# Attention on one Trainium2 core: where a group's first blocks and the multiply by the reciprocals stand

## The chip, the cores and the metric

The kernel runs on one core of a Trainium2 chip. Five engines work with queues of their own and meet at semaphores: TensorE (PE), VectorE (DVE), ScalarE (ACT), GpSimd (POOL) and SyncE (SP), which issues most DMAs. The metric is device time in microseconds (us), the median of several runs.

## The reference, cut to what matters

Three layers follow each other, each with a residual: half a mixture-of-experts feed-forward network, attention, and half a feed-forward network again. The change is in the attention.

```python
x = L0_attn_x                                     # (2, 2048, 512)
x = x + 0.5 * ffn(layernorm(x), ...)
x = x + attn(layernorm(x), Wq, bq, Wk, bk, Wv, bv, Wo, bo)
x = x + 0.5 * ffn(layernorm(x), ...)

def attn(x, ...):                                 # 16 query heads of 32, one head of keys and values
    q = (x @ Wq + bq).reshape(b, s, 16, 32).transpose(0, 2, 1, 3)
    k = x @ Wk + bk
    v = x @ Wv + bv
    scores = einsum('bhsd,btd->bhst', q, k) / sqrt(32)
    out = einsum('bhst,btd->bhsd', softmax(scores, axis=-1), v)
    return out.transpose(0, 2, 1, 3).reshape(b, s, 512) @ Wo + bo
```

## The kernel before

The attention works on 32 groups: 8 chunks of 512 queries (QT) by 4 groups (GPC) of 4 heads (HG). G counts the groups, g is the place in the chunk. For a group the keys come in 16 steps of 128 (STEPS), taken as 8 pairs (PAIRS).

What one group does:

- **PE, scores** (L1562): for each step and head a 128x512 matmul into one of three banks of pS. ACT takes the exponential of each (L1520) into prob. `scores` for the first step of a group waits until the shifts have been copied into qT.
- **PE, values** (L1600): for each step four matmuls into pO, when its four exponentials are done. The first of a group waits until pO has been copied out (semaphore s_oc).
- **POOL, pair sums** (L1461): adds the exponentials of two steps, and its DMAs (L1477) add these sums in acc. PE adds acc over the keys (`denominators`, pair 3).
- **The shifts.** A softmax needs the maximum of each row before the exponentials. While group G is computed, PE makes the score blocks of group G+1 a second time, in the other layout (`maxima`, L1575, 64 blocks of 128x512). I call them **blocks**. Each goes to one of the 4 banks of pM (RING), and DVE reduces it to its row maxima (L1716); PE may be four blocks ahead of DVE and no more. When all 64 are done, DVE makes the shifts (`make_shifts`, L1727 to L1731), PE transposes them into bank 2 of pM (`transposed_shifts`, L1591), and DVE and ACT copy two heads each into qT (`copy_shift`, L1738 and L1525). The third block of a group waits for these copies, since it reuses the bank.
- **The reciprocals.** DVE copies the sums out of PSUM (`copy_d`, pair 3, L1748). SP writes them to DRAM and reads them back as 128x16; DVE takes the reciprocals (`reciprocals`, behind the blocks of pair 5, RECIPROCAL_PAIR, L1754); SP writes them to DRAM and reads them back broadcast into d_rec, by four DMAs of 64 KB (L1399). All this is for the group before, G-1. Then POOL multiplies the copied values by d_rec (`normalise`, L1490), behind its last pair sum of the group.
- **The values' copy.** DVE copies pO (`copy_o`, L1743) at the start of the next group, behind its first two blocks (EARLY).
- **The output.** In the second group of each chunk but the first, PE multiplies the chunk before by Wo, in four parts behind pairs 1, 2, 4 and 6 (`output`, L1584), and DVE adds each to x (L1721). I call these the output groups; there are 7.

The order of PE is written out by hand. AT_HEAD says behind which of the first eight scores of a group a block stands (the first score comes with the seam), AT_PAIR how many blocks are among the eight scores issued in pair p, for the steps of pair p+1. EARLY blocks of a group come ahead of its first score, at the end of the group before. Each engine's queue is in order. So a waiting instruction holds everything behind it on its engine. `chunks` runs chunks 1 and 2, and chunks 4 to 6, as loops, and the others as straight code; the loops turn three times in all.

## Time and profile before

| | |
|---|---|
| median of 3 runs | 3292.02 us (3288.11 to 3294.11) |
| the profiled execution's own time | 3288.66 us |
| its span, first to last instruction | 3286.9 us |
| busy: PE, DVE, ACT, POOL | 2812.6, 2045.0, 1481.8, 2210.8 us |
| attention, transposes of the first group to the last's | from 833.0 to 2520.9 us |
| L1716, reductions of blocks (DVE) | 1984 of 680 ns, 1210.8 us busy |
| L1575 and L1562, blocks and scores (PE) | 1984 and 2048, 808.3 and 842.0 us busy |
| L1490, multiply by the reciprocals (POOL) | 31, 1302 ns the median |
| PE idle at the transposes (L1591), ended by DVE's shift | 17.1 us in 25 waits |
| POOL idle before L1490, ended by the DMA of d_rec | 19.2 us in 19 waits |

The span is cut into 40 slices on the page; slices 11 to 31 are the attention's. Busy matmuls overlap their neighbours in the records, so a distance between starts says more of PE than a duration. An idle time stands in brackets with what ended it: "[0.44 <-DVE attention_shift L1731]" is 0.44 us without work, ended by that instruction of DVE.

### The profile page before, as it was taken

What the parts mean: (1) busy time and instruction counts of PE and PEld (TensorE: products, weight loads), DVE (VectorE), ACT (ScalarE), POOL (GpSimd) and SP (SyncE); (2) the same over time, 40 slices, a digit from 0 to 9 for tenths busy, and PEclk for the clock granted to TensorE, in tenths of its full rate; (3) what the DMA queues carried; (4) which work ended last, traced back from release to release, by engine and by line L of the source; (5) the groups of instructions that cost most, each with busy time, mean ns of one, the idle gap of its engine ahead of it and who ended that gap; (6) DMA issues with size and microseconds to landing.
All of it is one profiled execution on the core that took longest, in us unless ns stands there. A gap on an engine that the chain in (4) does not pass through costs nothing. (4 is left out here: it accounts for less than half of the span.)

```text
span 3286.9 us, 50812 instructions
## 1 busy us (share of the span) xinstructions
PE 2812.6 (86%) x15136; PEld 1579.5 (48%) x15136; DVE 2045.0 (62%) x3940; ACT 1481.8 (45%) x2815; POOL 2210.8 (67%) x1392
## 2 busy tenths in 40 slices
PE   7967778398899999999999999999999798777760
PEld 4644444176555454555554544455554355444430
DVE  7943222267788787788787877777875397222222
ACT  3422222153666565566565655665656243222210
POOL 2148888462688787788887877877878222788870
PEclk9989887699999999999999999999999898879885
DMA  6479999894577676676776766757766243999998
GB/s 215 167 210 249 235 243 232 191 278 158 113 161 142 136 159 140 142 153 131 166 142 135 159 138 139 156 116 155 144 124 142 89 166 116 245 235 245 235 197 315
DMA packets 217011, 576.36 MB, mean 175 GB/s; under 512 B 33948, under 2 KB 34972, under 8 KB 192792
## 3 DMA queue, kind: packets, MB, share of 16 engines
q0 software_dynamic: 87296, 343.98, 52.0%
q1 hardware_dynamic: 125208, 220.55, 20.5%
q10 hardware_dynamic: 4224, 8.39, 0.7%
q8 instruction: 137, 2.24, 0.3%
q14 instruction: 146, 1.20, 0.1%
HBM read 230.94 MB, written 155.24 MB: 117 GB/s over the span
## 5 line engine op out<-in xcount | busy, mean ns | idle before, releaser
L1716 DVE TENSOR_REDUCE attention_mx<-attention_pM 128x1 f32<-128x512 f32 x1984 | 1210.8, 680 | 208.7 <-PE attention_pM L1575 192.6
L1520 ACT ACTIVATE attention_prob<-attention_pS 128x512 f32<-128x512 f32 x2048 | 1035.0, 631 | 565.9 <-PE attention_pS L1562 471.3
L1461 POOL TENSOR_TENSOR attention_pair<-attention_prob 128x1024 f32<-128x1024 f32 x380 | 949.5, 2507 | 195.6 <-ACT attention_prob L1520 184.0
L1562 PE MATMUL attention_pS<-attention_qT,prep_kT 128*128 128x512 f32 x2048 | 842.0, 417 | 25.3 <-issue 16.7
L1575 PE MATMUL attention_pM<-prep_kT,attention_qT 96*128 96x512 f32 x1984 | 808.3, 410 | 0.0
L1562 PEld LDWEIGHTS attention_pS<-attention_qT,prep_kT 128*128 128x128 f32 x2048 | 389.2, 191 | 365.8 <-issue 178.0
L1600 PE MATMUL attention_pO<-attention_prob,attention_v 128*32 128x512 f32 x4096 | 492.5, 598 | 0.0
L629 POOL DMA_INDIRECT sum<-experts_res,c_table x256 | 403.7, 1577 | 106.7 <-issue 76.6
L1575 PEld LDWEIGHTS attention_pM<-prep_kT,attention_qT 96*128 96x128 f32 x1984 | 378.5, 192 | 110.4 <-DVE attention_mx L1716 44.4
L755 DVE TENSOR_SCALAR experts_res<-experts_pD,experts_rows 128x512 f32<-128x512 f32 x128 | 90.7, 747 | 422.5 <-DMA sum<-experts_res,c_table 277.3
L658 PE MATMUL experts_pT<-c_ident,experts_rows 128*128 128x128 f32 x1024 | 186.3, 325 | 189.9 <-issue 69.4
L613 POOL DMA_INDIRECT experts_rows<-xn_rows,c_table x256 | 250.0, 976 | 103.0 <-issue 70.7
L658 PEld LDWEIGHTS experts_pT<-c_ident,experts_rows 128*128 128x128 f32 x1024 | 146.4, 211 | 235.5 <-issue 103.3
L1461 POOL TENSOR_TENSOR prep_acc<-attention_prob 128x1024 f32<-128x1024 f32 x68 | 165.2, 2582 | 132.1 <-ACT attention_prob L1520 132.1
L672 PE MATMUL experts_pU<-experts_xT,experts_wup 128*64 128x256 f32 x2048 | 245.6, 394 | 8.3 <-DVE experts_xT L739 8.1
L717 ACT ACTIVATE experts_res<-experts_pD,experts_rows 128x512 f32<-128x512 f32 x128 | 82.3, 684 | 321.1 <-DMA sum<-experts_res,c_table 281.0
L1600 PEld LDWEIGHTS attention_pO<-attention_prob,attention_v 128*32 128x32 f32 x4096 | 107.0, 109 | 244.1 <-issue 134.5
L672 PEld LDWEIGHTS experts_pU<-experts_xT,experts_wup 128*64 128x64 f32 x2048 | 148.0, 143 | 145.6 <-issue 84.7
L270 POOL TENSOR_TENSOR route_eqp<-route_eq,route_count 128x1536 f32<-128x1536 bf16 x16 | 52.1, 3259 | 212.5 <-ACT route_count L376 212.5
L685 PE MATMUL experts_pD<-experts_wdn,experts_hid 64*128 64x512 f32 x512 | 186.8, 866 | 4.8 <-DVE experts_hid L747 3.9
L739 DVE COPY experts_xT<-experts_pT 128x512 f32<-128x512 f32 x128 | 88.1, 688 | 158.5 <-PE experts_pT L658 88.9
L1461 POOL TENSOR_TENSOR attention_acc<-attention_prob 128x1024 f32<-128x1024 f32 x64 | 156.0, 2604 | 28.3 <-ACT attention_prob L1520 28.3
(161 smaller groups left out, 2695.2 us busy)
## 6 DMA issues: line engine op xcount, KB each, us to landing
prep_acc<-attention_pair POOLq DMA_DIRECT2D x96, 1024.0 KB, 7.7
attention_acc<-attention_pair POOLq DMA_DIRECT2D x90, 1024.0 KB, 7.6
experts_wup<-in_L_ffn_w_up_dram SPq DMA_DIRECT2D x128, 256.0 KB
attention_qT<-q_parts SPq DMA_DIRECT2D x96, 256.0 KB
xn_rows<-route_xn SPq DMA_DIRECT2D x16, 1152.0 KB, 6.7
sum<-route_sh SPq DMA_DIRECT2D x16, 1024.0 KB, 4.4
experts_wdn<-in_L_ffn_w_down_dram SPq DMA_DIRECT2D x64, 256.0 KB
q_parts<-prep_acc SPq DMA_DIRECT2D x64, 256.0 KB, 4.4
```

Of the source, the lines that this page charges most:

```text
L613: pool.indirect_dma_start(rows[e % RING][:, a * HALVES + h, :], None, xn_d, bass.IndirectOffsetOnAxis(ap=k["table"][:, 2 * e + a, h:h + 1] ...
L629: pool.indirect_dma_start(sums[a], bass.IndirectOffsetOnAxis(ap=k["table"][:, 2 * e + a, h:h + 1], axis=0), res[e % 2][:, a, h, :], None, ...
L658: t = pe.transpose(pT[:, half, o:o + P], rows[e % RING][:, a * HALVES + h, c:C:CK], k["ident"][:, :])
L672: t = pe.matmul(pU[b][a * H:(a + 1) * H, v, :], wup[b][:, a, c, v * H:(v + 1) * H], xT[b][:, c, a, :], start=c == 0, stop=c == CK - 1)
L685: pe.matmul(pD[:, h, a, :], hid[b][own, h * P:(h + 1) * P], wdn[b][own, :], start=True, stop=True).then_inc(s_dn[a], 1)
L755: dve.tensor_scalar(res[e % 2][:, 1, h, :], pD[:, h, 1, :], rows[e % RING][:, HALVES + h, C + 2 * e + 1:C + 2 * e + 2], None, ALU.mult).th ...
L1461: pool.tensor_tensor(to[:, part], prob[2 * n % PROBS][:, part], prob[(2 * n + 1) % PROBS][:, part], ALU.add).then_inc(s_pair, 1)
L1520: act.activation(prob[t % PROBS][:, h * QT:(h + 1) * QT], pS[:, at, :], ACT.Exp).then_inc(s_ex, 1)
L1562: pe.matmul(pS[:, at, :], kT[:, key:key + P], qT[g][:, h, :], start=True, stop=True).then_inc(s_sc, 1)
L1575: pe.matmul(pM[:, r % RING, :], qT[g][0:3 * DH, h, t * P:(t + 1) * P], kT[0:3 * DH, key:key + 512], start=True, stop=True).then_inc(s_mp, 1)
L1600: ins = pe.matmul(pO[h * DH:(h + 1) * DH, :], v_sb[:, batch * STEPS + t, :], prob[t % PROBS][:, h * QT:(h + 1) * QT], start=t == 0, stop=t ...
L1716: dve.tensor_reduce(mx[:, unit, part:part + 1], pM[:, r % RING, :], X, ALU.max).then_inc(s_mr, 1)
```

## The change

Three things change, in the attention alone.

1. The order of blocks. Four blocks (EARLY) stand ahead of a group's first score, two of them directly behind the transposes and so ahead of the last two steps' values, two behind these values. The head has four blocks and not six; pairs 4 and 5 have nine and pair 6 has six.
2. ACT copies the values (`copy_o`), between its copies of the shifts and the next group's first exponential.
3. DVE multiplies by the reciprocals (`normalise`), behind its copies of the shifts and ahead of the next group's first block. POOL does so no more.

The wait for Wo's load moves to its first use.

```diff
-        EARLY = 2
-        AT_HEAD = (0, 0, 1, 1, 1, 1, 1, 1)
-        AT_PAIR = (8, 8, 8, 8, 8, 8, 8, 0)
+        EARLY = 4
+        AT_HEAD = (0, 0, 0, 0, 1, 1, 1, 1)
+        AT_PAIR = (8, 8, 8, 8, 9, 9, 6, 0)
...
@@ gpsimd
-                            if last and n == STEPS // 2 - 2:
-                                normalise(c, g - 1)
...
-                            normalise(c, g - 1)
...
@@ scalar
+                def copy_o(G, g):
+
+                    act.wait_ge(s_pv, A + (G + 1) * STEPS)
+                    act.activation(o_raw(g)[:, :], pO[:, :], ACT.Copy).then_inc(s_oc, 1)
...
                             for h in (2, 3):
                                 copy_shift(G + 1, (g + 1) % GPC, h)
+                            copy_o(G, g)
                             for h in range(HG):
                                 exponential(G + 1, 0, h)
...
@@ tensor
                             two_steps(0, 2 * p + 2, () if last else range(AT_PAIR[p]))
+                            if not last and AT_PAIR[p] > 2 * HG:
+                                maxima(base, r, n, nxt, ahead, G)
+                                n, r = n + 1, r + 1
                         elif not last:
 
                             transposed_shifts(G + 1)
+                            if not before_last:
+                                early(*follower, range(2))
...
-                            early(c + 1 if nxt == 0 else c, nxt, 1 if end else ahead)
+                            early(*follower, range(2, EARLY))
                         scores(G + 1, nxt, 0, 0, ahead)
...
@@ vector
+                def normalise(c, g):
+
+                    G = GPC * c + g
+                    dve.wait_ge(s_oc, A + G + 1)
+                    dve.wait_ge(s_ri, A + 64 * (G + 1))
+                    dve.tensor_tensor(o_n[g][:, :], o_raw(g)[:, :], d_rec[:, :], ALU.mult).then_inc(s_on, 1)
...
-                    if not first:
-                        copy_o(c if g else c - 1, (g - 1) % GPC)
...
                         make_shifts(G + 1, base + r)
                         for h in range(2):
                             copy_shift(G + 1, (g + 1) % GPC, h)
+                    if not first:
+                        normalise(c if g else c - 1, (g - 1) % GPC)
```

PE at the seam between two groups, before. L1575 are blocks (pM), L1562 scores (pS), L1600 values (pO), L1591 the transposes:

```order
L1562 MATMUL attention_pS<-attention_qT,prep_kT 128x512
L1575 MATMUL attention_pM<-prep_kT,attention_qT 128x512
L1600 MATMUL attention_pO<-attention_prob,attention_v 32x512 x8
L1591 MATMUL attention_pM<-c_ident,attention_shift 128x128 x4
L1600 MATMUL attention_pO<-attention_prob,attention_v 32x512 x8
L1575 MATMUL attention_pM<-prep_kT,attention_qT 128x512 x2
L1562 MATMUL attention_pS<-attention_qT,prep_kT 128x512 x3
L1575 MATMUL attention_pM<-prep_kT,attention_qT 128x512
```

The same place now (the lines are L1561, L1548, L1587 and L1578):

```order
L1548 MATMUL attention_pS<-attention_qT,prep_kT 128x512 x2
L1587 MATMUL attention_pO<-attention_prob,attention_v 32x512 x8
L1578 MATMUL attention_pM<-c_ident,attention_shift 128x128 x4
L1561 MATMUL attention_pM<-prep_kT,attention_qT 128x512 x2
L1587 MATMUL attention_pO<-attention_prob,attention_v 32x512 x8
L1561 MATMUL attention_pM<-prep_kT,attention_qT 128x512 x2
L1548 MATMUL attention_pS<-attention_qT,prep_kT 128x512 x5
L1561 MATMUL attention_pM<-prep_kT,attention_qT 128x512
```

The last scores ahead of the transposes have no blocks between them, two blocks come ahead of the last values and two behind, and five scores follow without a block.

DVE from the copy of the sums of one group to that of the next, before:

```order
L1748 COPY attention_d<-attention_pM 128x512
L1716 TENSOR_REDUCE attention_mx<-attention_pM 128x1 x16
L1754 RECIPROCAL attention_d_in<-attention_d_in 128x16
L1716 TENSOR_REDUCE attention_mx<-attention_pM 128x1 x8
L1727 TENSOR_REDUCE attention_pM<-attention_mx 128x16
L1728 TENSOR_REDUCE attention_shift<-attention_mx 128x16
L1731 TENSOR_TENSOR attention_shift<-attention_pM,attention_shift 128x16
L1738 CAST attention_qT<-attention_pM 32x512 x2
L1716 TENSOR_REDUCE attention_mx<-attention_pM 128x1 x2
L1743 COPY attention_o_n<-attention_pO 128x512
L1716 TENSOR_REDUCE attention_mx<-attention_pM 128x1 x38
```

And now:

```order
L1737 COPY attention_d<-attention_pM 128x512
L1710 TENSOR_REDUCE attention_mx<-attention_pM 128x1 x18
L1743 RECIPROCAL attention_d_in<-attention_d_in 128x16
L1710 TENSOR_REDUCE attention_mx<-attention_pM 128x1 x6
L1721 TENSOR_REDUCE attention_pM<-attention_mx 128x16
L1722 TENSOR_REDUCE attention_shift<-attention_mx 128x16
L1725 TENSOR_TENSOR attention_shift<-attention_pM,attention_shift 128x16
L1732 CAST attention_qT<-attention_pM 32x512 x2
L1750 TENSOR_TENSOR attention_o_n<-attention_o_n,attention_d_rec 128x512
L1710 TENSOR_REDUCE attention_mx<-attention_pM 128x1 x40
```

Six reductions and not eight stand between the reciprocals and the shifts; the copy behind the next group's second block is gone, and the multiply with d_rec stands ahead of all of that group's reductions.

## Rows read from the trace of the kernel before

**Rows 1.** The page: the clock granted to PE in 40 slices, in tenths.

```profile
PEclk9989887699999999999999999999999898879885
```

**Rows 2.** Timeline, PE: start, us, engine, line, operation, count, idle before and releaser.

```profile
2355.96 0.66 PE L1591 MATMUL attention_pM<-c_ident,attention_shift 128*128 128x128 f32 x4 [0.43 <-DVE attention_shift L1731]
...
2394.03 0.51 PE L1562 MATMUL attention_pS<-attention_qT,prep_kT 128*128 128x512 f32 x1
...
2397.97 1.92 PE L1600 MATMUL attention_pO<-attention_prob,attention_v 128*32 128x512 f32 x16
2399.83 0.50 PE L1562 MATMUL attention_pS<-attention_qT,prep_kT 128*128 128x512 f32 x1
...
2403.77 1.92 PE L1600 MATMUL attention_pO<-attention_prob,attention_v 128*32 128x512 f32 x16
2406.13 0.66 PE L1591 MATMUL attention_pM<-c_ident,attention_shift 128*128 128x128 f32 x4 [0.44 <-DVE attention_shift L1731]
...
2409.15 0.86 PE L1562 MATMUL attention_pS<-attention_qT,prep_kT 128*128 128x512 f32 x3
...
2410.23 0.51 PE L1562 MATMUL attention_pS<-attention_qT,prep_kT 128*128 128x512 f32 x1
...
2417.45 1.07 PE L1600 MATMUL attention_pO<-attention_prob,attention_v 128*32 128x512 f32 x8
```

**Rows 3.** Timeline, DVE, in the same group.

```profile
2399.60 0.24 DVE L1754 RECIPROCAL attention_d_in<-attention_d_in 128x16 f32<-128x16 f32 x1
2400.60 4.87 DVE L1716 TENSOR_REDUCE attention_mx<-attention_pM 128x1 f32<-128x512 f32 x8 [0.76 <-PE attention_pM L1575]
...
2405.89 0.18 DVE L1731 TENSOR_TENSOR attention_shift<-attention_pM,attention_shift 128x16 f32<-128x16 f32 x1
2406.83 1.40 DVE L1738 CAST attention_qT<-attention_pM 32x512 fp32r<-32x512 f32 x2 [0.75 <-PE attention_pM L1591]
2409.11 1.29 DVE L1716 TENSOR_REDUCE attention_mx<-attention_pM 128x1 f32<-128x512 f32 x2 [0.88 <-PE attention_pM L1575]
2410.32 0.68 DVE L1743 COPY attention_o_new<-attention_pO 128x512 f32<-128x512 f32 x1
```

**Rows 4.** Timelines of three groups: reciprocals (DVE), last pair sum and multiply (POOL).

```profile
1302.71 0.24 DVE L1754 RECIPROCAL attention_d_in<-attention_d_in 128x16 f32<-128x16 f32 x1
1314.24 1.30 POOL L1490 TENSOR_TENSOR attention_o_n<-attention_o_n,attention_d_rec 128x512 f32<-128x512 f32 x1 [1.68 <-DMA attention_d_rec<-d_parts]
...
1518.00 0.24 DVE L1754 RECIPROCAL attention_d_in<-attention_d_in 128x16 f32<-128x16 f32 x1
1527.51 1.39 POOL L1490 TENSOR_TENSOR attention_o_n<-attention_o_n,attention_d_rec 128x512 f32<-128x512 f32 x1
...
2406.59 2.67 POOL L1461 TENSOR_TENSOR attention_pair<-attention_prob 128x1024 f32<-128x1024 f32 x1
2409.75 1.30 POOL L1490 TENSOR_TENSOR attention_o_n<-attention_o_n,attention_d_rec 128x512 f32<-128x512 f32 x1 [0.48 <-DMA attention_d_rec<-d_parts]
2412.90 2.39 POOL L1461 TENSOR_TENSOR attention_acc<-attention_prob 128x1024 f32<-128x1024 f32 x1 [1.85 <-ACT attention_prob L1520]
```

**Rows 5.** Timelines of an output group: reciprocals (DVE) and transposes (PE).

```profile
1794.29 0.24 DVE L1754 RECIPROCAL attention_d_in<-attention_d_in 128x16 f32<-128x16 f32 x1
...
1803.91 0.66 PE L1591 MATMUL attention_pM<-c_ident,attention_shift 128*128 128x128 f32 x4
```

**Rows 6.** Windows behind a loop turn: stretch, length, PE busy, PEclk, DMA, GB/s.

```profile
1254.80:1261.60 6.80, 3.45 (x8) 0.50 0.81 157
1261.60:1265.10 3.50, 1.82 (x8) 0.99 0.01 2
1265.10:1268.50 3.40, 3.40 (x10) 0.50 0.00 0
```

**Rows 7.** Timelines of the stage before, a DVE and a POOL addition.

```profile
659.72 1.73 POOL L1033 TENSOR_TENSOR attentionp_got<-attentionp_got,prep_bo 128x512 f32<-128x512 f32 x1
660.88 1.14 DVE L1162 TENSOR_TENSOR attentionp_got<-attentionp_got,attentionp_other 128x512 f32<-128x512 f32 x1
```

More of the change, by code:

```diff
@@ L1432, in _ @@
             def _(pool):
-                begin(pool, s_pair, s_on)
+                begin(pool, s_pair)
                 def add_pair(c, g, n):
@@ L1478, in bring @@
                                    ).then_inc(s_acc[g % 2][n % 2], 16)
-                def normalise(c, g):
-                    G = GPC * c + g
-                    pool.wait_ge(s_oc, A + G + 1)
-                    pool.sem_inc(k["pool_on"], 1)
-                    pool.wait_ge(s_ri, A + 64 * (G + 1))
-                    pool.sem_inc(k["pool_on"], 1)
-                    if g == 0 and not (isinstance(c, int) and c == 0):
-                        pool.wait_ge(s_mr, A + items_before(c, 2))
-                        pool.sem_inc(k["pool_on"], 1)
-                    pool.tensor_tensor(o_n[g][:, :], o_raw(g)[:, :], d_rec[:, :], ALU.mult).then_inc(s_on, 1)
                 def body(c, batch):
@@ L1496, in body @@
                             add_pair(c, g, n)
-                            if last and n == STEPS // 2 - 2:
-                                normalise(c, g - 1)
-                        if last:
-                            continue
-                        if g > 0:
-                            normalise(c, g - 1)
-                        elif not (isinstance(c, int) and c == 0):
-                            normalise(c - 1, GPC - 1)
                 chunks(body)(pool)
@@ L1509, in _ @@
             def _(act):
-                begin(act, s_ex, s_sha)
+                begin(act, s_ex, s_oc, s_sha)
                 def exponential(G, t, h):
@@ L1581, in output @@
                     if t == 0:
+                        pe.wait_ge(s_wo, A + 16)
                         pe.wait_ge(s_on, A + GPC * (c + 1))
@@ L1634, in last_output, with early @@
                         ins.then_inc(s_mp, 1)
-                def early(c, g, ahead):
+                def early(c, g, ahead, blocks):
                     nxt = (g + 1) % GPC
                     pe.wait_ge(s_q[nxt], A + 48 * (c + (2 if nxt == 0 else 1)))
-                    for n in range(EARLY):
+                    for n in blocks:
                         maxima(items_before(c, g), n, n, nxt, ahead, GPC * c + g)
@@ L1651, in group @@
                     ahead = 1 if static and c == CHUNKS // 2 - 1 and nxt == 0 else batch
+                    before_last = static and c == CHUNKS - 1 and nxt == GPC - 1
+                    turn = static and c == CHUNKS // 2 - 1 and nxt == GPC - 1
+                    follower = (c + 1 if nxt == 0 else c, nxt, 1 if turn else ahead)
                     base = items_before(c, g)
@@ L1682, in group @@
                     if not last:
-                        if not (static and c == CHUNKS - 1 and nxt == GPC - 1):
-                            end = static and c == CHUNKS // 2 - 1 and nxt == GPC - 1
-                            early(c + 1 if nxt == 0 else c, nxt, 1 if end else ahead)
+                        if not before_last:
+                            early(*follower, range(2, EARLY))
                         scores(G + 1, nxt, 0, 0, ahead)
@@ L1693, in _ @@
                 transposed_shifts(0)
-                early(0, 0, 0)
+                early(0, 0, 0, range(EARLY))
                 scores(0, 0, 0, 0, 0)
-                pe.wait_ge(s_wo, A + 16)
                 chunks(body)(pe)
@@ L1710, in _ @@
             def _(dve):
-                begin(dve, s_mr, s_mx, s_shift, s_shd, s_dc, s_rec, s_oc, s_lrec, s_lon)
+                begin(dve, s_mr, s_mx, s_shift, s_shd, s_dc, s_rec, s_on, s_lrec, s_lon)
                 def maxima(base, r, n):
@@ L1738, in copy_shift @@
                     dve.tensor_copy(qT[g][3 * DH:4 * DH, h, :], pM[h * DH:(h + 1) * DH, 2, :]).then_inc(s_shd, 1)
-                def copy_o(c, g):
-                    dve.wait_ge(s_pv, A + (GPC * c + g + 1) * STEPS)
-                    dve.tensor_copy(o_raw(g)[:, :], pO[:, :]).then_inc(s_oc, 1)
                 def copy_d(base, r, G):
```

## The prediction, made before the changed kernel was timed

> **What bounds the kernel now.** I read the page first. TensorE (PE) is busy nine tenths or more of nearly every slice of the attention stage, and its clock is 0.9 to 1.0 there [rows 1]. So I looked for PE's idle time and asked who ends it, by the timeline of one group.
>
> A group has 64 score matmuls and 64 "blocks" (matmuls for the next group's row maxima, each of which DVE must reduce), eight pairs of steps, and a seam. I measure everything from the shifts' transposes, called T. They start at 2355.96 and 2406.13: 50.17 us a group [rows 2]. A pair of steps takes 5.80 us (2394.03 to 2399.83): 3.94 for 16 matmuls, or 0.24 an item, and 1.86 for the values (2397.97 to 2399.83). DVE needs (4.87 - 0.68) / 7 = 0.60 us for a reduction in a row of eight [rows 3], so a pair costs it 4.8: PE is the bound there and DVE catches up during the values.
>
> Two places are different.
> - At T, PE waits. Its last values start at 2403.77 and take 1.86, so it could transpose at 2405.63; it does so at 2406.13, 0.50 later, idle until DVE's shift [rows 2, 3].
> - Behind T, DVE is the bound. Values 14 and 15, two blocks and the first score come by T + 3.02. DVE starts on the blocks at T + 2.98 (2409.11), copies the values at 2410.32, and the next values of PE start at T + 11.32 (2417.45) [rows 2, 3]. PE is four blocks ahead at most (the ring), so those values come when DVE is through 12 reductions and the copy: 13 turns of 0.60 after 2409.11 is 2416.9, and another 0.5 for the last block and the switch. The row says 8.34 from DVE's first reduction to PE's values.
>
> **The change, part by part.**
>
> *Blocks out of the last pair.* Two fewer at pair 6, one more at each of pairs 4 and 5. PE's sum stays. Before T, both engines shift: PE starts pair 6 at 2399.83 + 0.24 and is at T after 3.94 - 0.48 + 1.86, at 2405.39. DVE begins pair 6's reductions at 2400.60 + 0.24 and needs six: 5 x 0.60 + 0.68 to 2404.5, then 0.60 for the shifts (2405.48 to 2406.07) [rows 3]: 2405.1. The shifts are ready in time and the 0.50 wait goes. The ninth block costs no wait: its ring place is free after five reductions.
>
> *The reciprocals slide towards T.* DVE takes them behind pair 5's ninth reduction: 0.60 later, 2400.20. So T is 5.2 us behind them, not 6.5 (2399.60 to 2406.13).
>
> *The multiply goes from POOL to DVE, behind the shift copies and ahead of all blocks.* This decides. The multiply waits for four transfers that SP issues once the reciprocals are done, through DRAM. POOL's multiply starts 10.15 us behind them in this group, 0.48 of it waiting for that DMA; the earliest of the ordinary groups is 9.51 (1518.00 to 1527.51), the latest 11.53 (1302.71 to 1314.24) [rows 4]. Over the 19 ordinary groups that have blocks behind the seam (not behind an output group, not at a loop's turn) the mean is 10.37. POOL could afford that. DVE has its shift copies done at T + 2.1 (2408.23) [rows 3] and then stands until T + 10.37 - 5.2 = T + 5.2, with two, then four blocks waiting in PSUM. The multiply takes a turn of 0.60, taken from the copy of the same size that it replaces; DVE's first reduction starts at T + 5.8, against T + 2.98.
>
> PE passes four blocks unhindered (the ring), and four scores without blocks. Its fifth block needs one reduction done, at T + 5.8 + 0.68, and PE is there at T + 3.02 + 0.48 (two more items) + 1.08 (2409.15 to 2410.23) + 0.48 + 0.24 = T + 5.3: it waits some 1.2 us, and from there on DVE paces it. The next values need 12 reductions and now no copy: 8.34 - 0.60 = 7.74 behind the first, T + 13.5. That is 2.2 us later than 11.32. Less the 0.50 at T, an ordinary group loses 1.7 us; 19 x 1.7 = **+32 us**. No later pair gives it back, since PE bounds those.
>
> *Seven seams in output groups.* There the output's matmuls lie between, so T is 9.62 us behind the reciprocals (1794.29 to 1803.91) [rows 5]. Now 8.8 (0.60 less, and 0.24 less of PE). With the ordinary groups' 9.5 to 11.5 the multiply could start at T + 0.7 to T + 2.7, and DVE asks for it at T + 2.1. DVE would allow the values at T + 2.7 + 7.74 = 10.4; An exponential, and with it a score, comes each 0.48 at best (PE's two items; from a score to the next there ACT is no faster), so score 15 comes at T + 3.5 + 1.08 + 12 x 0.48 and the values 0.66 later (the last block, and the switch), at T + 11.0: 0.3 gained. T itself had no wait there. 7 x 0.3 = -2.
>
> *Three loop turns.* Behind such a seam PE is busy 3.45 of 6.8 us, and the clock is at 0.50 [rows 6]: it stands on the branch and then runs at half speed, which hides DVE's delay. Only the wait at T goes: -1.5. The first seam has no multiply (-0.9). The last seam has no blocks: the 0.50 goes, and ACT's copy gives it back.
>
> *ACT's copy of the values.* 0.6 us, between the shift copies and the next exponential. The last values end near T + 3.4 and the first exponential is at T + 3.4 (2409.58) today, T + 3.9 then: hidden at the cost of at most 0.1, taken as nothing. It takes the copy off DVE, which is counted above.
>
> *POOL's multiply (1.3 us) goes.* POOL then waits for ACT 1.85 us anyway [rows 4]: nothing.
>
> *Interference of DVE and POOL.* A DVE addition of two 128x512 SBUF tiles takes 1.14 us beside POOL's addition of the same shape [rows 7]; DVE's copy of that shape takes 0.68 [rows 3]. Were the multiply beside POOL's additions it would cost 0.46 more, 9 us over 19 groups. But POOL's last addition ends at T + 3.1 and its next starts at T + 6.8 (2406.59 + 2.67, 2412.90) [rows 4], and DVE's multiply is at T + 5.2: I take nothing, and 9 for the upper end. The Trainium skill ("GPSIMD Engine Reference", Key points) says that POOL shares its SBUF interfaces with VectorE and contends with a DVE instruction that has two SBUF inputs, which the multiply is. By that alone the sum would be 9 us more; the trace agrees with the rule, and says that at this place POOL rests.
>
> *The clock.* The stretch 1261.60 to 1265.10, in which PE waited for ACT and was busy 1.82 of 3.5 us, had 0.99; the next 3.4 us had 0.50, the lower level of 1.2 GHz [rows 6]. The new wait at the fifth block is 1.2 us on average and 2.3 in the latest group. In six of the 19 groups it is over 1.4. A stretch of 3.4 us at half speed costs 1.7, of which DVE's pace hides about 1.0. I add 6 x 0.7 = +4; the ends are 0 and 19 x 1.7 = 32.
>
> Sum: 32 - 2 - 1.5 - 0.9 + 4 = **+31.6 us** on the profiled execution's 3288.66, so 3320. The median shown is 3.4 above that execution; within the runs' own spread of 6, I leave 3320.
>
> **The rivals.**
> - *The data is there in time* (faster). If the transfers landed by T + 3.3, which is 8.5 behind the reciprocals, DVE would be no later than today plus the 0.50 gained. Were they there by T + 2.1, all 19 groups would gain 0.50 + 0.3, 15 us, and with the rest 20 us: 3269. For it: the last transfer is 64 KB, and POOL's own big DMAs, which share the engines, may fall otherwise. Against it: the earliest of 19 is 9.51, and though it is only an upper bound where POOL came later than the data, 13 of the 19 did wait for the DMA. Chance 0.11.
> - *Break-even*: the chain shortens by about 1.5 us and the rest cancels: 3293 or so, within 0.2% (6.6 us, about what a measurement here can tell). Chance 0.08.
> - *The clock falls in every ordinary group*: +28 + 32, or 3348. For it: PE works in gaps for 8 us behind each seam. Against it: today's waits of 0.5 us and DVE's pace at the seam leave 1.0. Chance 0.17.
> - My forecast as worked out: 0.64.
> - That DVE does not really stand there would need a multiply behind the blocks in DVE's row; the order shows it ahead of 40 reductions.
>
> **How the numbers follow.** The landing's uncertainty of 0.7 us either way gives 19 x 0.7 = 13 us, the clock 0 to 32, POOL 9. Downwards 3307, stretched to 3298 for part of the break-even; upwards 3348 for the clock in every group. Faster 0.11, same 0.08, slower 0.81.
>
> **What would show it.** In the changed profile: DVE idle before its multiply until the DMA of d_rec, some 3 us in each of 22 seams, 60 to 70 in all; PE idle at the transposes gone (0.44 a group today); the distance from T to the next values 13 to 14 us in ordinary groups and 11 in output groups; ordinary groups 51.9 us long, output groups 0.3 us shorter than before. I am wrong if DVE's multiply starts by T + 3.3, or if the ordinary group is at 50.2 or less. If the distance is right and the total is over 3335, it is the clock: the granted clock in the ordinary groups then shows it.

## The result, and the profile after

| | before | changed |
|---|---|---|
| median of 4 runs, us | 3290.07 | 3332.03 |
| lowest to highest, us | 3286.00 to 3294.11 | 3328.89 to 3333.54 |
| profiled execution and its span, us | 3288.66, 3286.9 | 3328.89, 3327.2 |

The ratio of the times is 1.0127, with a 95% interval of 1.0114 to 1.0139: 42 us slower. 3320 was forecast, with a range of 3298 to 3348. The measured time lies inside it, and the sign is right.

The page's row of the clock, to be held against [rows 1]:

```profile
PEclk9988889699999999999999999999999899788885
```

The attention stage is at 0.9 throughout, as before, so the loss isn't one of the clock. From the first T of the stage to its last the profiled execution took 1724.4 us, against 1687.6: 36.8 of the 40.2 us by which the two profiled executions differ. T is the start of the shifts' transposes, as in the prediction. PE's timeline over one ordinary group, as [rows 2] showed it:

```profile
2088.70 1.92 PE L1587 MATMUL attention_pO<-attention_prob,attention_v 128*32 128x512 f32 x16
...
2096.90 1.92 PE L1587 MATMUL attention_pO<-attention_prob,attention_v 128*32 128x512 f32 x16
...
2103.10 1.92 PE L1587 MATMUL attention_pO<-attention_prob,attention_v 128*32 128x512 f32 x16
...
2108.66 1.92 PE L1587 MATMUL attention_pO<-attention_prob,attention_v 128*32 128x512 f32 x16
2110.52 0.66 PE L1578 MATMUL attention_pM<-c_ident,attention_shift 128*128 128x128 f32 x4
...
2113.99 0.85 PE L1548 MATMUL attention_pS<-attention_qT,prep_kT 128*128 128x512 f32 x3
2115.21 0.99 PE L1548 MATMUL attention_pS<-attention_qT,prep_kT 128*128 128x512 f32 x2 [0.37 <-ACT attention_prob L1500]
...
2122.91 1.06 PE L1587 MATMUL attention_pO<-attention_prob,attention_v 128*32 128x512 f32 x8
```

T is at 2110.52. It comes 1.86 us behind the start of the last values ahead of it (2108.66), without the 0.50 of waiting that stood in [rows 2]. The next values start at T + 12.39, where [rows 2] had T + 11.32. DVE in the same group:

```profile
2104.91 0.25 DVE L1743 RECIPROCAL attention_d_in<-attention_d_in 128x16 f32<-128x16 f32 x1
2105.72 3.68 DVE L1710 TENSOR_REDUCE attention_mx<-attention_pM 128x1 f32<-128x512 f32 x6 [0.56 <-PE attention_pM L1561]
...
2111.22 1.40 DVE L1732 CAST attention_qT<-attention_pM 32x512 fp32r<-32x512 f32 x2 [1.21 <-PE attention_pM L1578]
2113.74 1.40 DVE L1750 TENSOR_TENSOR attention_o_n<-attention_o_n,attention_d_rec 128x512 f32<-128x512 f32 x1 [1.12 <-DMA attention_d_rec<-d_parts]
2115.17 3.68 DVE L1710 TENSOR_REDUCE attention_mx<-attention_pM 128x1 f32<-128x512 f32 x6
```

DVE has its shift copies done at 2112.62 and stands until 2113.74 for the DMA. Its first reduction starts at T + 4.65, against T + 2.98 in [rows 3]. The multiply takes 1.40 us. A copy of that shape took 0.68 [rows 3], and the forecast gave the multiply 0.60. POOL, beside it:

```profile
2109.01 2.37 POOL L1461 TENSOR_TENSOR attention_pair<-attention_prob 128x1024 f32<-128x1024 f32 x1 [0.65 <-ACT attention_prob L1500]
2111.32 0.85 POOL L1477 DMA_DIRECT2D prep_acc<-attention_pair  x1
2111.91 2.67 POOL L1461 TENSOR_TENSOR attention_pair<-attention_prob 128x1024 f32<-128x1024 f32 x1
2117.94 2.39 POOL L1461 TENSOR_TENSOR attention_acc<-attention_prob 128x1024 f32<-128x1024 f32 x1 [3.36 <-ACT attention_prob L1500]
```

POOL's addition ends at 2114.58, and DVE's multiply at 2115.14, 0.56 later. That distance comes back below.

DVE's waits for the DMA, in the profile's list of waits (idle us, times, longest), sum to what was forecast (60 to 70):

```profile
DVE attention_o_n L1750 <- DMA attention_d_rec<-d_parts: 62.1, 24, 7.3
```

But 14.4 of these 62.1 us are two waits, one in the fifth seam (7.1) and one in the last group (7.3). In the 18 ordinary seams that are left DVE stood for 33.8 us, 1.9 each, where some 3 had been forecast.

The seams against those of the profile before, summed. A seam is from T to the next values (those of the next group), the rest is from those values to the next T. The first two seams, which have no multiply, lost nothing (-0.7 together).

| | seams, us | rest, us |
|---|---|---|
| 18 ordinary groups | +24.4 | +5.5 |
| the ordinary group with T at 1036.45 | +7.8 | +0.3 |
| 7 output groups | -0.4 | +1.4 |
| 3 loop turns | -2.7 | +1.2 |

One ordinary seam stands out, the fifth:

```profile
1031.77 0.25 DVE L1743 RECIPROCAL attention_d_in<-attention_d_in 128x16 f32<-128x16 f32 x1 [0.69 <-DMA attention_d_in<-d_parts]
...
1045.65 0.69 DVE L1750 TENSOR_TENSOR attention_o_n<-attention_o_n,attention_d_rec 128x512 f32<-128x512 f32 x1 [7.10 <-DMA attention_d_rec<-d_parts]
```

The data came 13.9 us behind the reciprocals there, and DVE stood for 7.10 us. PE's next block waited 5.12 us for DVE, and the clock was at 0.50 from 1043.2 on for 10.2 us, the only ordinary seam where it fell. So the loss has three parts: some 24 us spread over 18 seams, about 1.4 each; 8 in one seam; and 6 or so in the pairs. The turns' -2.7 is not read as a gain: in the eleven later profiles the three turn seams together stood from -2.9 to +2.7 against those before, and from -2.7 to +2.7 where the order of the blocks was the changed one.

### The profile page after: what moved, and what is told of

Same layout as the page of the kernel before. It is cut to its first block and busy times, and to the rows that moved or that the text cites. A ratio compares the mean times of both kernels' runs of the same rounds, so it can differ in the third digit from the quotient of the medians.

```text
span 3327.2 us, 50783 instructions
## 1 busy us (share of the span) xinstructions
PE 2843.7 (85%) x15136; PEld 1577.9 (47%) x15136; DVE 2069.4 (62%) x3940; ACT 1510.8 (45%) x2846; POOL 2170.7 (65%) x1361
## 5 line engine op out<-in xcount | busy, mean ns | idle before, releaser
L1548 PE MATMUL attention_pS<-attention_qT,prep_kT 128*128 128x512 f32 x2048 | 841.3, 419 | 32.2 <-issue 19.3
L1561 PE MATMUL attention_pM<-prep_kT,attention_qT 96*128 96x512 f32 x1984 | 813.7, 417 | 12.2 <-DVE attention_mx L1710 8.4
L1548 PEld LDWEIGHTS attention_pS<-attention_qT,prep_kT 128*128 128x128 f32 x2048 | 388.6, 190 | 370.2 <-issue 179.9
L1587 PE MATMUL attention_pO<-attention_prob,attention_v 128*32 128x512 f32 x4096 | 492.5, 598 | 0.0
L1561 PEld LDWEIGHTS attention_pM<-prep_kT,attention_qT 96*128 96x128 f32 x1984 | 374.0, 191 | 159.9 <-DVE attention_mx L1710 95.4
L1587 PEld LDWEIGHTS attention_pO<-attention_prob,attention_v 128*32 128x32 f32 x4096 | 106.9, 109 | 243.7 <-issue 152.1
```

The lines of the kernel that those rows point to most:

```text
L1548: pe.matmul(pS[:, at, :], kT[:, key:key + P], qT[g][:, h, :], start=True, stop=True).then_inc(s_sc, 1)
L1561: pe.matmul(pM[:, r % RING, :], qT[g][0:3 * DH, h, t * P:(t + 1) * P], kT[0:3 * DH, key:key + 512], start=True, stop=True).then_inc(s_mp, 1)
L1587: ins = pe.matmul(pO[h * DH:(h + 1) * DH, :], v_sb[:, batch * STEPS + t, :], prob[t % PROBS][:, h * QT:(h + 1) * QT], start=t == 0, stop=t ...
```

## The experiments

The baseline of each run is the kernel before on the same chip: 3288.3 for e1 to e4, 3287.3 for e5 to e8, 3270.97 for e9 and e10. Ratios are to that. Edits are against the changed kernel. "POOL multiplies" means that POOL's multiply and its waits of before are back and DVE's is gone, with everything else left as changed. The chip of e9 and e10 is faster outside the attention (their first T comes at 826, not at 833, and behind the last T they take 756 and 759 us, not 766), so that their times in us are not to be held against 3290: times 3290, their ratios give 3319 and 3272.

### e1: the changed kernel again

> The changed kernel once more, for its fifth seam (T at 1036.45 in its profile). There DVE's multiply started 9.2 us behind the transposes, because two small DMAs of the reciprocals' chain took over 6 us and not 1.7, and the clock fell behind it: 8 us of the loss of 42. Theory 'a collision that depends on the moment': the profile of this run has it in another seam, or in none, and the time varies by up to 8 us with it. Theory 'fixed by the program': the fifth seam has it again, with the values 19 us behind the transposes. Time 3325 to 3335 by both.

Measured: 3324.92, ratio 1.0107 (1.0087 to 1.0127). The 18 ordinary seams were at +25.6, the rest at +5.2, as before. The fifth seam was at +1.0 and not at +7.8. The even part repeats, and the outlier depends on the execution; how small a difference decides it is shown below, with the fifth seam.

### e2: DVE's multiply behind the first pair's blocks

```diff
-                    if not first:
-                        normalise(c if g else c - 1, (g - 1) % GPC)
...
+                        if p == 0 and not first and not (static and c == 0 and g == 1):
+                            normalise(c if g > 1 else c - 1, (g - 2) % GPC)
```

> The multiply stays on DVE, but stands behind the blocks of pair 0 of the next group; all else as changed. Theory A (DVE stands at the seam for the DMA of d_rec, with the blocks behind it): DVE's first reduction starts 2.1 to 2.3 us behind the transposes in every seam and the values 11.0 to 11.3 behind them, as in today's output seams; the 24 us of the 18 ordinary seams and the 8 of the fifth go: 3297 to 3301. Theory B (the loss is in the new order of the blocks or in ACT's copy): 3325 or more. The rest of the group (39.2 us from the first values to the next transposes) stays by both.

Measured: 3456.51, ratio 1.0512 (1.0494 to 1.0529): a clear miss. The seams did go back to those of before (0 in sum), but the rest grew by 107 us in the ordinary groups and 47 in the output groups. DVE's instructions grouped by line (busy us, mean ns, idle before), over the stage, in e2:

```profile
L1750 DVE TENSOR_TENSOR attention_o_n<-attention_o_n,attention_d_rec 128x512 f32<-128x512 f32 x22 | 104.7, 4758 | 1.7 <-DMA attention_d_rec<-d_parts 1.7
```

The data was there (1.7 us of idle in 22), and yet the multiply lasted 4.76 us on average, and 5.0 to 5.4 in nearly all groups. One of them, DVE's timeline of e2 and then POOL's:

```profile
1968.76 5.42 DVE L1750 TENSOR_TENSOR attention_o_n<-attention_o_n,attention_d_rec 128x512 f32<-128x512 f32 x1
1974.10 2.47 DVE L1710 TENSOR_REDUCE attention_mx<-attention_pM 128x1 f32<-128x512 f32 x4
```

```profile
1966.32 7.30 POOL L1461 TENSOR_TENSOR attention_acc<-attention_prob 128x1024 f32<-128x1024 f32 x3
```

POOL's three additions end at 1973.62, the multiply at 1974.18, 0.56 behind them. So DVE's multiply did not run slowly beside POOL; it did not run until POOL stopped. The theory that only the DMA matters falls with this run. The 154 us are not the multiply alone: the granted clock, which before was at 0.50 for 34 us of the stage, all at loop turns, now was there for 3.4 us or more in every group but the first two and the last, 173 us in all.

### e3: POOL multiplies

> The multiply goes back to POOL; the order of blocks and ACT's copy stay as changed. Theory A: as with the multiply late on DVE, 3296 to 3301, since DVE never waits for the DMA and has one turn less of 0.6 us, which no one waits for. Theory B: 3325 or more. If the time is clearly under the 3290 of the kernel before, the order and ACT's copy are a gain of their own; by the changed kernel's rows (ninth blocks cost 0.3 to 0.4 us each, the wait at the transposes of 0.5 is gone) I expect the rest of a group 0.2 us longer than before and the seam 0.1 shorter, so 3290 to 3297 is as likely.

Measured: 3303.69, ratio 1.0046 (1.0033 to 1.0059). By the ratios the multiply's place on DVE accounts for about 27 of the 42 us (0.0081 of 3290), and 15 remain with the new order; against e1, on the same chip, it is 21. The executions of e3 spread from 3296.80 to 3308.09, and the profiled one is among the fastest (3297.69): it lost 9.7 us between the first T and the last, 4.6 of them at the loop turns. What makes the others slower isn't known. The ordinary seams were at -1.1, the rest of the ordinary groups at +6.1, the turn seams at +2.7. The order by itself therefore buys nothing at the seam, though DVE has no copy any more. ACT's timeline of e3 in a group with T at 2086.83:

```profile
2089.86 0.60 ACT L1531 ACTIVATE attention_o_n<-attention_pO 128x512 f32<-128x512 f32 x1 [1.14 <-PE attention_pO L1607]
2090.86 7.95 ACT L1520 ACTIVATE attention_prob<-attention_pS 128x512 f32<-128x512 f32 x16 [0.40 <-PE attention_pS L1568]
```

The exponentials start at T + 4.03, because four blocks stand ahead of the first score, and then come one per 0.48 us. 15 of these steps lead to T + 11.2, and the values stand at T + 11.3: the seam had become ACT's.

### e4: the reciprocals a pair earlier

```diff
-RECIPROCAL_PAIR = 5
+RECIPROCAL_PAIR = 4
```

> The changed kernel with the reciprocals one pair earlier (behind pair 4's blocks). The chain of DMAs then has some 5 us more. Theory A: the data is there when DVE has copied the shifts, the multiply starts 2.1 us behind the transposes, and the ordinary seams are like the output seams (values at 11.3): 3299, plus up to 0.5 us a group (15) since DVE now waits some 1.6 us for d_in (it lands 4.6 us ahead of today's reciprocals, pair 4's last reduction ends 6.2 ahead): 3299 to 3314. Theory B: 3325 or more.

Measured: 3341.54, ratio 1.0155 (1.0138 to 1.0172): slower than the changed kernel, not faster. The ordinary seams still lost 18.9 us, and the rest 21.9. Two things had not been reckoned with.

The first is the chain. The reciprocals came 5.5 us earlier against T, but the data only 0.6 to 2.4 (at T + 1.9 to T + 3.8, and not T + 3.2 to T + 5.1), since it landed 12.8 to 14.9 us behind the reciprocals. In an ordinary group, with T at 2122.32, SP's issues of that chain in e4:

```profile
2109.66 0.35 SPq L1390 DMA_DIRECT2D attention_d_in<-d_parts  x1
2111.52 0.35 SPq L1393 DMA_DIRECT2D d_parts<-attention_d_in  x1
2116.79 3.26 SPq L1399 DMA_DIRECT2D attention_d_rec<-d_parts  x4
```

The loads wait for the write of the reciprocals to land, 5.3 us here; in the profile before it was 1.4 to 1.8 in most groups. The reciprocals now also stood for their own input, 1.4 to 1.8 us of DVE in the middle of a pair that PE paces. A chain through DRAM does not land as much earlier as it is started.

The second is POOL. In this group the data was there at T + 1.9, ahead of DVE's shift copies, so DVE waited for nothing. DVE's timeline, then POOL's:

```profile
2124.45 2.50 DVE L1750 TENSOR_TENSOR attention_o_n<-attention_o_n,attention_d_rec 128x512 f32<-128x512 f32 x1
```

```profile
2123.72 2.68 POOL L1461 TENSOR_TENSOR attention_pair<-attention_prob 128x1024 f32<-128x1024 f32 x1
```

The multiply ended at T + 4.63, 0.55 behind POOL's addition, and the values came at T + 12.40. In all 18 groups it ended at T + 4.5 to T + 4.7, whenever the data had landed. So this run did take away the DMA's part of the seams (24.4 to 18.9), and what is left is POOL's addition, as e9 shows without any DMA.

### e5: DVE's multiply behind the four early blocks

```diff
+                    if not first and not (static and c == 0 and g == 1):
+                        normalise(c if g > 1 else c - 1, (g - 2) % GPC)
```

with the call at the seam gone (but for the last group's) as in e2; it stands right behind the loop over the EARLY blocks.

> The multiply stays on DVE, behind the four early blocks of the next group (all else as changed). With the multiply behind pair 0's blocks the time was 3456.5, since DVE's multiply lasted 5.4 us there beside three additions of POOL. Theory C (DVE's multiply of two SBUF tiles does not run while POOL adds, and ends 0.6 us behind POOL's last addition): here it falls in POOL's pause (about 4.1 to 7.3 us behind the transposes), lasts 0.7 us nearly everywhere, and the ordinary seams have their values 11.3 to 12 us behind the transposes: 3298 to 3310. Theory D (the multiply behind blocks costs as such, by the DMA or by the order of waits): the multiply is long here too, and the time over 3340.

Measured: 3301.73, ratio 1.0046 (1.0028 to 1.0064), the time of e3. The ordinary seams were at -1.1, the rest at +5.3, and the fifth seam was late once more (+6.0). The same operation of the same engine, some 2.4 us later in its queue, in e5:

```profile
L1750 DVE TENSOR_TENSOR attention_o_n<-attention_o_n,attention_d_rec 128x512 f32<-128x512 f32 x23 | 16.1, 701 | 11.7 <-DMA attention_d_rec<-d_parts 11.6
```

The changed kernel has in that view

```profile
L1750 DVE TENSOR_TENSOR attention_o_n<-attention_o_n,attention_d_rec 128x512 f32<-128x512 f32 x23 | 36.6, 1591 | 59.8 <-DMA attention_d_rec<-d_parts 59.8
```

Behind the early blocks the multiply falls into POOL's pause, where it takes 0.70 us, and the data is nearly always there.

### e6: the order of before, POOL multiplies, ACT copies the values

```diff
-        EARLY = 4
-        AT_HEAD = (0, 0, 0, 0, 1, 1, 1, 1)
-        AT_PAIR = (8, 8, 8, 8, 9, 9, 6, 0)
+        EARLY = 2
+        AT_HEAD = (0, 0, 1, 1, 1, 1, 1, 1)
+        AT_PAIR = (8, 8, 8, 8, 8, 8, 8, 0)
...
-                                early(*follower, range(2))
...
-                            early(*follower, range(2, EARLY))
+                            early(*follower, range(EARLY))
```

> The kernel before with one part of the change alone: ACT copies the values. The blocks stand as before and POOL multiplies. With the changed order and POOL's multiply (3303.7) the seam was bound by ACT, whose exponentials start 4.05 us behind the transposes and come every 0.48; with two early blocks they start at 3.59, and ACT's copy (2.6 to 3.2) fits ahead of them. DVE has one turn of 0.6 less. Theory 'DVE's turn was the bound at the seam': values 10.8 to 10.9 us behind the transposes and not 11.3, 29 seams by 0.45: 3275 to 3279. Theory 'the copy on ACT costs what it gives': 3287 to 3293.

Measured: 3278.38, ratio 0.9975 (0.9965 to 0.9984), 8 us faster than before. The ordinary seams were at -7.2, the output groups' at -2.8, the rest at 0. ACT's copy is the one part of the change shown to gain by itself. PE's timeline of e6:

```profile
2070.05 0.66 PE L1598 MATMUL attention_pM<-c_ident,attention_shift 128*128 128x128 f32 x4 [0.42 <-DVE attention_shift L1743]
...
2081.03 1.92 PE L1607 MATMUL attention_pO<-attention_prob,attention_v 128*32 128x512 f32 x16
```

and ACT's:

```profile
2073.64 7.95 ACT L1520 ACTIVATE attention_prob<-attention_pS 128x512 f32<-128x512 f32 x16 [0.41 <-PE attention_pS L1568]
```

T + 10.98 in place of T + 11.32, with the exponentials from T + 3.59. The wait of 0.42 at T is still there.

### e7: e3 with eight blocks in every pair

```diff
-        AT_PAIR = (8, 8, 8, 8, 9, 9, 6, 0)
+        AT_PAIR = (8, 8, 8, 8, 8, 8, 8, 0)
```

With EARLY 4 and the pairs at eight, the same 64 blocks stand as four ahead of a group's first score, four among its first eight scores and 56 in the pairs.

> As the run with the multiply on POOL (3303.7), but pairs 4, 5 and 6 have eight blocks again; four early blocks, two of them behind the transposes, stay. Theory 'the ninth blocks cost more than the wait at the transposes': pair 4 falls from 8.1 to 7.6 us and pair 5 from 6.2 to 5.8, pair 6 rises from 5.5 to 5.8 and the 0.5 of wait at the transposes is back; the rest of a group falls from 39.2 to 39.0: 5 to 8 us less, 3288 to 3299. Theory 'the moved blocks are a gain': 3304 or more.

Measured: 3290.23, ratio 1.0018 (1.0008 to 1.0027). So the 15 us of e3 fall into two: the ninth blocks account for 9 (1.0046 to 1.0018), and against e6 four early blocks in place of two for 14 (1.0018 to 0.9975; the medians are 12 apart). PE's timeline of e7:

```profile
2049.70 1.92 PE L1607 MATMUL attention_pO<-attention_prob,attention_v 128*32 128x512 f32 x16
2055.49 1.92 PE L1607 MATMUL attention_pO<-attention_prob,attention_v 128*32 128x512 f32 x16
2063.18 1.92 PE L1607 MATMUL attention_pO<-attention_prob,attention_v 128*32 128x512 f32 x16
2068.97 1.92 PE L1607 MATMUL attention_pO<-attention_prob,attention_v 128*32 128x512 f32 x16
```

Pair 4, with the denominators' matmuls, is 7.69 us long there and pair 5 is 5.79. With nine blocks they are 8.20 (2088.70 to 2096.90) and 6.20 (to 2103.10) in the changed kernel: 0.51 and 0.41 for one block each. Pair 6 with six blocks gave back only 0.23 (5.56).

### e8: e6 with 9 and 7 blocks in the last two pairs

```diff
-        AT_PAIR = (8, 8, 8, 8, 8, 8, 8, 0)
+        AT_PAIR = (8, 8, 8, 8, 8, 9, 7, 0)
```

> The kernel before with ACT's copy, and one block moved from pair 6 to pair 5 (8, 8, 8, 8, 8, 9, 7, 0). By the changed kernel's rows the ninth block costs pair 5 0.39 us, pair 6 gets 0.15 to 0.24 shorter, and the wait at the transposes falls from 0.5 to about 0.1: 0.1 to 0.2 us less a group than with ACT's copy alone, 3 to 5 us, 3271 to 3276. If the ninth block costs as much as the wait gave, it is within 2 us of that run.

Measured: 3276.27, ratio 0.9971 (0.9960 to 0.9981). The seams were those of e6 (-7.1), the rest at -2.1 over the ordinary groups, 0.12 a group. The wait at T goes, and the ninth block takes most of it back. Against e6 the intervals overlap, so that a gain of 2 to 4 us rests on the profiles alone.

### e9: no wait for the DMA

```diff
-                    dve.wait_ge(s_ri, A + 64 * (G + 1))
-                    dve.tensor_tensor(o_n[g][:, :], o_raw(g)[:, :], d_rec[:, :], ALU.mult).then_inc(s_on, 1)
+                    dve.tensor_tensor(o_n[g][:, :], o_raw(g)[:, :], null[:, :], ALU.mult).then_inc(s_on, 1)
```

> The changed kernel, but DVE multiplies the values by a tile of zeros and does not wait for d_rec (so the attention adds only its bias; the chain of DMAs still runs). It parts the seam's loss in two. Theory C (DVE's multiply does not run beside POOL's addition): in ordinary seams the multiply starts 2.1 us behind the transposes, lasts until POOL's last addition has ended at 4.06, and DVE's first reduction is at 4.6, the values at 12.3 to 12.4: as in today's best seams. The seams of 12.8 to 13.6, the fifth and what follows them fall to that: 3332 - 5 - 8, 3317 to 3322. Theory A alone (the DMA is all of it): the first reduction at 2.9, the values at 11.3, 3298 to 3302.

This kernel leaves out the division: it multiplies by zeros. Measured: 3299.91, ratio 1.0089 (1.0073 to 1.0104), or 3319 on the scale of the other chips. That is theory C's range; that the bare number is near theory A's comes from the faster chip. With no DMA to wait for, 29 of the 42 us are still there. The 18 ordinary seams were at +19.0, each with the values at T + 12.33 to T + 12.41; the fifth was like the others (+1.0). DVE's timeline of e9, with T at 2093.55, and POOL's:

```profile
2094.24 1.40 DVE L1733 CAST attention_qT<-attention_pM 32x512 fp32r<-32x512 f32 x2 [1.19 <-PE attention_pM L1579]
2095.67 2.49 DVE L1750 TENSOR_TENSOR attention_o_n<-attention_o_n,attention_null 128x512 f32<-128x512 f32 x1
2098.20 9.06 DVE L1711 TENSOR_REDUCE attention_mx<-attention_pM 128x1 f32<-128x512 f32 x15
```

```profile
2094.95 2.66 POOL L1462 TENSOR_TENSOR attention_pair<-attention_prob 128x1024 f32<-128x1024 f32 x1
2100.97 2.39 POOL L1462 TENSOR_TENSOR attention_acc<-attention_prob 128x1024 f32<-128x1024 f32 x1 [3.36 <-ACT attention_prob L1501]
```

The multiply starts at T + 2.12, as soon as DVE is free, and ends at 2098.16, 0.55 behind POOL's addition (2097.61). Its first reduction is at T + 4.65, as in the changed kernel's group above. In the output groups POOL's addition had ended at T + 0.5, the multiply took 0.69, and the values came at T + 11.31.

### e10: one early block

From e3, with

```diff
-        EARLY = 4
-        AT_HEAD = (0, 0, 0, 0, 1, 1, 1, 1)
-        AT_PAIR = (8, 8, 8, 8, 9, 9, 6, 0)
+        EARLY = 1
+        AT_HEAD = (0, 1, 1, 1, 1, 1, 1, 1)
+        AT_PAIR = (8, 8, 8, 8, 8, 9, 7, 0)
...
-                                early(*follower, range(2))
+                                early(*follower, range(1))
...
-                            early(*follower, range(2, EARLY))
```

> ACT's copy, POOL's multiply, pairs of 8, 8, 8, 8, 8, 9, 7, and one early block instead of two, standing behind the transposes. The seam with two early blocks is bound by ACT (exponentials from 3.59 us on, values at 10.8 to 11.0). One block fewer ahead of the scores starts them 0.24 earlier, and DVE's first reduction is at 2.1: values at 10.6 to 10.75, 29 seams by 0.2: 3269 to 3273. If ACT's copy, which then ends only at 3.4, holds the first exponential, nothing is gained: 3275 to 3278.

Measured: 3252.87, ratio 0.9944 (0.9931 to 0.9958), or 3272 on the scale of the other chips: 18 us faster than before, and the best of all. Every ordinary seam and every output seam was 10.83 us long. PE's timeline of e10, then ACT's:

```profile
2059.58 0.66 PE L1598 MATMUL attention_pM<-c_ident,attention_shift 128*128 128x128 f32 x4
2059.99 0.47 PE L1581 MATMUL attention_pM<-prep_kT,attention_qT 96*128 96x512 f32 x1
...
2070.42 1.92 PE L1607 MATMUL attention_pO<-attention_prob,attention_v 128*32 128x512 f32 x16
```

```profile
2062.92 7.95 ACT L1520 ACTIVATE attention_prob<-attention_pS 128x512 f32<-128x512 f32 x16
```

The exponentials start at T + 3.34, 0.69 before those of e3. From the first T to the last it is 17.3 us shorter than before (1670.3 against 1687.6), and 3.4 shorter than e8, which differs in the number and place of the early blocks alone; by the ratios that step is 9.

## Why the prediction was right, and where its steps failed

**Right in the number and in who pays, wrong in what DVE stands for.** DVE stands at the seam with the next group's blocks behind it, and PE pays at the next values. The wait at T went (0.50). e3 and e5 show that it is the multiply at that place: taken away, or put 2.4 us later, it gives back 20 to 27 us. But the forecast put all of DVE's standing down to the DMA, and most of it is POOL. The prediction had said that it was wrong if the multiply started by T + 3.3: in three of the 18 groups it did, in three more by T + 3.35, and these seams still were 12.33 to 12.41 us long, because POOL's addition held the multiply. So much of the agreement of 3320 with 3332 is luck.

**"Interference of DVE and POOL: I take nothing."** This step failed, and it is the main one. It failed twice. POOL's last addition was read in the old order, where it ended at T + 3.1; in the new one T comes earlier against it, and it ends at T + 4.06. And the size was misread. The DVE addition of 1.14 us in [rows 7] ran from 660.88 to 662.02, and POOL's from 659.72 to 661.45: it ended 0.57 behind POOL's. I had taken 0.46 as a fixed price of running side by side. It was the rest of POOL's addition, so the price is however much POOL has in a row: 0.69 us became 1.40, 2.49 (e9), 5.42 (e2). The Trainium skill has the rule ("SBUF — State Buffer", Who interferes with whom): a DVE instruction with two SBUF inputs and a GpSimd instruction that reads SBUF exclude one another, and the second to issue blocks until the first is through. The traces agree, with 0.55 to 0.57 us from POOL's end to DVE's (POOL waiting for DVE is seen in no run here). They add that DVE did not get in between adjacent POOL instructions (e2: three of them).

**The landing of the data: too late.** I took it 10.37 us behind the reciprocals, from when POOL's multiply began. It was 8.7 to 10.7 in the ordinary groups, 9.5 on average. That 10.37 was an upper bound explains little of it: in the profile before, the data itself landed 9.3 to 11.4 behind the reciprocals, 10.2 on average, so the chain was 0.7 quicker in the new order. The data was therefore at T + 3.9 on average, at T + 5.1 in two groups and at T + 3.2 or T + 3.3 in six. The two errors cancel: without the DMA (e9) the ordinary seams lose 19.0 of the 24.4, so POOL's addition is the floor, and the DMA adds 5 and the fifth seam's 7. Values at T + 12.33 to T + 13.6, mean +1.36, stand against a forecast of +2.2.

**"The ninth block costs no wait."** Failed: 0.51 and 0.41 where 0.24 each was taken, and 0.23 saved at pair 6 where 0.48 was. The rest of the group was then +0.30, not -0.50 (in e7, without the ninth blocks, it was 0.0). 1.36 + 0.30 = 1.66 for an ordinary group, against 1.7 in the sum: again two errors of opposite sign. The other terms: 7 output groups +1.0 in place of -2, the turns -1.5 as forecast but within their scatter of some 3, the first seam 0 in place of -0.9, the clock nothing in the 18 groups in place of +4, and the fifth group +8.1, which the forecast did not have. The distance from the reciprocals to T was 5.5 to 5.6 for the 5.2 worked out, for the same reason.

**Output seams, -0.3 each.** The mechanism was right (ACT sets them), the size was off: -0.05, as the exponentials start at T + 4.05 and not at T + 3.9.

**ACT's copy "taken as nothing".** Right inside the changed kernel, wrong as a statement on the copy: alone it gains 8 us (e6), since it takes 0.60 off DVE at the place where DVE is the bound. What hides the gain is the two further blocks ahead of the scores, which delay ACT by 0.44 (T + 3.59 to T + 4.03).

**The clock, +4 with 32 as its end.** No ordinary seam but the fifth fell to 0.50. PE's waits at the fifth block were 0.91 us at most, below the 2.3 I had feared for the latest group.

**The fifth seam**, some 7 us, was not foreseen. In the changed kernel's profile SP's read of the denominators took 6.61 us to land there, so the reciprocals were late, and their write took 6.13:

```profile
1025.14 0.34 SPq L1390 DMA_DIRECT2D attention_d_in<-d_parts  x1
1032.04 0.34 SPq L1393 DMA_DIRECT2D d_parts<-attention_d_in  x1
1038.19 3.48 SPq L1399 DMA_DIRECT2D attention_d_rec<-d_parts  x4
```

POOL had issued a large accumulating DMA ahead of each, at 1024.60 and here:

```profile
1031.00 0.85 POOL L1477 DMA_DIRECT2D attention_acc<-attention_pair  x1
```

POOL's two transfers landed at 1031.55 and 1038.01, SP's two at 1031.74 and 1038.18. The twelve profiles hold 744 of these small reads and writes, and they agree. Of the 38 that were issued 0.5 to 4 us behind an issue of POOL's, 36 landed 7.1 us or more behind it, with POOL's transfer. Of the 706 others, 615 landed within 1.9 us and all but two within 3.8. So a small transfer that comes too late behind a large one waits for it. In e1 the same read was issued 0.51 us behind POOL's issue and landed in 1.60; in the changed kernel it was 0.54, in e2, e4 and e5 0.52 to 0.56, and it took 6.6 each time. The same holds for e4's writes: moved by the earlier reciprocals to 1.9 to 2.4 us behind POOL's issue, they took 4.8 us and more in every ordinary group but the fifth. No run moved POOL's issue alone.

**The rivals.** The condition of "the data is there in time", T + 3.3, was met in six of the 18 groups, and it did not bring a gain, because POOL's addition stood in its place. None of the rivals named that. "The clock falls in every ordinary group" did not happen here; it is what happened in e2.

Where the 42 us come from, one step after the other, by the ratios and by the profiles from the first T to the last without the loop turns:

| step | by the ratios, us | by the profiles, us |
|---|---|---|
| ACT's copy (before to e6) | -8 | -11 |
| four early blocks for two (e6 to e7) | +14 | +9 |
| the ninth blocks (e7 to e3) | +9 | +7 |
| the multiply on DVE, held by POOL's addition (e3 to e9) | +14 | +22 |
| the wait for the DMA (e9 to the changed kernel) | +13 | +11 |

In the last row 7 us are the fifth seam's, which in e1 was not late. The steps were taken in this order alone, and the two columns tell how well each is known.

## What to carry to other kernels

An elementwise operation with two SBUF inputs that moves to DVE must be placed in a pause of POOL, and the pause must be read in the new order, not the old one. An operation that waits for a DMA does not belong ahead of work that PE waits for: the same multiply behind four blocks cost 20 to 27 us less. At a seam, count what stands ahead of the slowest engine's first instruction: a copy moved off the bound engine gained 8 us here (e6), and one early block in place of two most of the further 10 (e10). And keep small DMAs of a chain off the microseconds behind the issue of a large one.

## What the runs showed of the hardware that was not expected

- DVE's 128x512 fp32 multiply from SBUF waited for POOL's additions of SBUF tiles to end, and ended 0.55 to 0.57 us behind them, whether one was running or three. In the last group of the changed kernel it lasted 17 us. DVE's timeline, and then POOL's:

```profile
2567.42 17.13 DVE L1750 TENSOR_TENSOR attention_o_n<-attention_o_n,attention_d_rec 128x512 f32<-128x512 f32 x1 [7.29 <-DMA attention_d_rec<-d_parts]
```

```profile
2567.34 7.33 POOL L1461 TENSOR_TENSOR attention_acc<-attention_prob 128x1024 f32<-128x1024 f32 x3
2574.34 9.65 POOL L1461 TENSOR_TENSOR attention_pair<-attention_prob 128x1024 f32<-128x1024 f32 x4
2584.61 4.71 POOL L1461 TENSOR_TENSOR attention_pair<-attention_prob 128x1024 f32<-128x1024 f32 x2 [0.63 <-ACT attention_prob L1500]
```

  It ended at 2584.55, in POOL's first gap of 0.6 us behind 2583.99. It cost nothing there: the first matmul of the last output came 53.9 us behind the last T, against 53.8 before.
- DVE's reductions from PSUM kept their pace of 0.60 us each (e9's row of 15), an addition of POOL's beside some of them.
- A small DMA of SP's issued 0.5 to 4 us behind POOL's 1 MB DMA landed with it, 7.1 us or more behind POOL's issue (36 of 38); issued less than 0.5 us behind, it took 1.4 to 1.9 us in 518 of 578.
- Starting a chain of small DMAs 5.5 us earlier brought its data 0.6 to 2.4 us earlier (e4).
